# Feed-forward stage: POOL takes over the last norm's variances, and ACT applies the norm two blocks later

## The chip, the cores and the metric

The kernel runs on one core of a Trainium2 chip. It is one program of 54,028 instructions on five engines that run side by side and meet through semaphores: PE (matrix multiply), DVE (vector), ACT (activation), POOL (GpSimd) and SP, which here only issues transfers. The metric is the device time of one execution in microseconds (us). Three runs of the kernel before gave 1488.28, 1488.96 and 1490.38 us, median 1488.96.

## The reference

A decoder layer on 64 sequences of 64 tokens with 256 channels (4096 tokens): self-attention, cross-attention and a feed-forward part, each added to the residual and followed by a layer norm. Only the feed-forward part and the last norm matter here:

```python
def _quant_act(x):
    scale = jnp.maximum(jnp.max(jnp.abs(x), axis=-1, keepdims=True), EPS) / 127.0
    xq = jnp.clip(jnp.round(x / scale), -128.0, 127.0) * scale
def bitlinear(x, w):                      # _quant_weight: ternary weights
    return jnp.einsum('bsi,oi->bso', _quant_act(x), _quant_weight(w))
gate = jax.nn.sigmoid(bitlinear(x, w_gate))   # 256 -> 1024
up = bitlinear(x, w_up)
h = gate * up
return bitlinear(h, w_down)                   # 1024 -> 256
# then: x = _layernorm(x + ffn(x)), v = var(x), (x - m) / sqrt(v + 1e-5)
```

## The kernel before

`feed_forward` is the last stage of the program. It works on 32 blocks of 128 tokens (NB = 32), one token per partition. X holds the residual, `X[:, e, :]` is block e, 128x256 in f32. There is no loop on the chip: every engine has its own straight list of instructions, written slot by slot. Slot n handles block n in its first step and earlier blocks in the later steps. What an engine does in a slot, in this order (line numbers are those of the kernel before):

- PE: `gP` and `uP` of block n (L1501), the down projection `xprojP` of block n-3 (L1511), the transposes `hmP` of block n-2 (L1520).
- ACT: `sig` of block n (L1543), `ds` = scaled down projection of n-3 (L1549), `hqT` of n-2 (L1554), and the last norm of an older block in place, `X*rstd + shift` (L1568). The list NORMED says which: block n-10, and in the last slot, 35, what is left of blocks 0 to 27.
- DVE: `hs` = up times gate of block n (L1644), its maximum `hsc` (L1647), the reciprocal `hinv` (L1649), and for block n-4 the statistics of the last norm, `bn_stats` (L1679) and `bn_aggr` (L1681). `bn_stats` leaves six numbers per token: count, mean and sum of squared deviations for two halves of the row; `bn_aggr` makes mean and variance of them (`ln_moments`).
- POOL: the residual add `X` for block n-3 (L1592); for block n the clipped reciprocal `hinv` (L1595), the quantised hidden row `hm` (L1598), the scale `hsc` (L1599) and the down scale `dsc` (L1601). Some slots have more: 1, 2, 12 and 13 have two `f_xs` each (L1617), slot 5 has the four small steps of the norm before (L1605 to L1610), and every fourth slot from 7 on calls `roots` for a group of four blocks.

`roots(m)` of group m, blocks 4m to 4m+3, stands in slot 4m+7, at its end. It has four instructions on 128x4 tiles: variance plus eps (L1578), power -0.5 (L1580), minus the mean (L1582), times the root (L1585). The groups 0 to 6 are blocks 0 to 27. The blocks 28 to 30 (group 7) and 31 (group 8) are done at the end, with only the first two instructions, and DVE applies their norm (L1692).

SP issues one output transfer for a group, in order of the groups (L1634): each waits for the norm of its whole group, and the ones behind it wait for SP.

Double buffers tie the engines together: `hs` of block n waits for `hm` of block n-2, the POOL's `hinv` of block n waits for DVE's reciprocal of block n, `hmP` waits for `hm`, and `uP` of block n waits for `hs` of block n-1.

Of the kernel before, what the change touches and what calls it, by code (L numbers as in the profile page):

```python
# [5 lines left out]
F32 = mybir.dt.float32  # L6
# [1438 lines left out]
def feed_forward(nc, X, ffn, projP, out, sem, sb, part):  # L1445
# [9 lines left out]
    tP = [part.enter_context(nc.psum_tensor(n, [P, DFF], F16)) for n in ("hmP0", "hmP1")]  # L1455
    dP = [projP[:, i * TILE:(i + 1) * TILE] for i in range(2)]
    s_g, s_u, s_t, s_dn = (sem("f_" + n) for n in ("g", "u", "t", "dn"))
    s_sig, s_h, s_max, s_sc, s_inv, s_dsc, s_hm, s_te, s_ds, s_y = (sem("f_" + n) for n in (
        "sig", "h", "max", "sc", "inv", "dsc", "hm", "te", "ds", "y"))
    s_stats, s_mom, s_rstd, s_normed, s_out = (sem("f_" + n) for n in ("stats", "mom", "rstd", "normed", "out"))  # L1460
    GROUP = 4
    groups = [slice(i, i + GROUP) for i in range(0, NB - GROUP, GROUP)] + [slice(NB - GROUP, NB - 1), slice(NB - 1, NB)]
# [26 lines left out]
    with nc.Block() as block:  # L1489
# [45 lines left out]
        @block.scalar  # L1535
        def _(act):
            def slot(n, has):
                if n == NB - PB:
                    wait(act, s_last, GUSC)
                if has(0):  # L1540
                    wait(act, s_g, n + 1)
                    wait(act, s_h, n - 1)
                    nc.scalar.activation(sig[:, n % 2, :], gP[:, :], ACT.Sigmoid, scale=gsc[:, n:n + 1]).then_inc(s_sig, 1)  # L1543
                if has(3) and n - 3 < LATE:
                    e = n - 3
                    wait(act, s_dn, e + 1)
# [13 lines left out]
                if 6 <= n < 6 + PB:  # L1560
                    i = NB - PB + n - 6
                    x = X[:, i, :]
                    wait(act, s_lastp, SHIFT)
                    nc.scalar.activation(x, x, ACT.Identity, bias=shift[:, i:i + 1], scale=rstd[:, i:i + 1]).then_inc(s_xqT, 1)
                for e in NORMED[n]:
                    x = X[:, e, :]
                    wait(act, s_shift, e // GROUP + 1)
                    nc.scalar.activation(x, x, ACT.Identity, bias=shift[:, e:e + 1], scale=rstd[:, e:e + 1]).then_inc(s_by_act, 1)  # L1568

            NORMED = [[e for e in range(MAIN) if min(e + 10, NB + 3) == n] for n in range(NB + 4)]  # L1570
            blocks(slot, 4)

        @block.gpsimd
        def _(pool):
            def roots(m):
                own = groups[m]
                wait(pool, s_mom, own.stop)
                nc.gpsimd.tensor_scalar(rstd[:, own], moments[:, own, 1], EPS, None, ALU.add).then_inc(s_small, 1)  # L1578
                wait(pool, s_small, 2 * m + 2 - max(0, m - MAIN // GROUP))
                nc.gpsimd.tensor_tensor(rstd[:, own], rstd[:, own], power[:, 0:own.stop - own.start], ALU.pow).then_inc(s_rstd, 1)  # L1580
                if own.stop <= MAIN:
                    nc.gpsimd.tensor_scalar(shift[:, own], moments[:, own, 0], -1.0, None, ALU.mult).then_inc(s_small, 1)  # L1582
                    wait(pool, s_small, 2 * m + 3)
                    wait(pool, s_rstd, m + 1)
                    nc.gpsimd.tensor_tensor(shift[:, own], shift[:, own], rstd[:, own], ALU.mult).then_inc(s_shift, 1)  # L1585

            def slot(n, has):
                if has(3) and n - 3 < LATE:
                    e = n - 3
                    wait(pool, s_ds, e + 1)  # L1590
                    x = X[:, e, :]
                    nc.gpsimd.tensor_tensor(x, ds[:, e % 2, :], x, ALU.add).then_inc(s_y, 1)  # L1592
                if has(0):
                    wait(pool, s_inv, n + 1)
                    nc.gpsimd.tensor_scalar(hinv[:, n:n + 1], hinv[:, n:n + 1], 1.0 / EPS, 127.0, ALU.min, ALU.mult).then_inc(s_sc, 1)  # L1595
                    wait(pool, s_sc, 2 * n + 1)
                    wait(pool, s_t, n - 1)
                    nc.gpsimd.tensor_scalar(hm[:, n % 2, :], hs[:, n % 2, :], hinv[:, n:n + 1], MAGIC16, ALU.mult, ALU.add).then_inc(s_hm, 1)  # L1598
                    nc.gpsimd.tensor_scalar(hsc[:, n:n + 1], hsc[:, n:n + 1], EPS, 1.0 / 127.0, ALU.max, ALU.mult).then_inc(s_sc, 1)  # L1599
                    wait(pool, s_sc, 2 * n + 2)  # L1600
                    nc.gpsimd.tensor_tensor(dsc[:, n:n + 1], hsc[:, n:n + 1], wsc[:, 2:3], ALU.mult).then_inc(s_dsc, 1)  # L1601
                if n == 5:
                    own = last_tile
                    wait(pool, s_last, MOM[PB - 1])
                    nc.gpsimd.tensor_scalar(rstd[:, own], moments[:, own, 1], EPS, None, ALU.add).then_inc(s_lastp, 1)  # L1605
                    nc.gpsimd.tensor_scalar(shift[:, own], moments[:, own, 0], -1.0, None, ALU.mult).then_inc(s_lastp, 1)
                    wait(pool, s_lastp, EPS2)
                    nc.gpsimd.tensor_tensor(rstd[:, own], rstd[:, own], power[:, :], ALU.pow).then_inc(s_lastp, 1)
                    wait(pool, s_lastp, ROOT)
                    nc.gpsimd.tensor_tensor(shift[:, own], shift[:, own], rstd[:, own], ALU.mult).then_inc(s_lastp, 1)  # L1610
                for k, tile in enumerate(XS_AT):
                    if n in XS_AT[tile]:
                        wait(pool, s_last, XINV if k else 0)
                        first = XS_AT[tile].index(n) * PB // 2
                        for b in range(first, first + PB // 2):
                            i = tile * PB + b
                            nc.gpsimd.tensor_scalar(xs[:, k, b, :], X[:, i, :], xinv[:, i:i + 1], MAGIC16, ALU.mult, ALU.add).then_inc(s_lastp, 1)  # L1617
                for m in range(NG):
                    if n - 4 == groups[m].stop - 1:
                        roots(m)  # L1620

# [123 lines left out]
```

## Time and profile before

| | us |
|---|---|
| median of three runs | 1488.96 |
| time of the profiled execution | 1488.86 |
| its span (first to last event) | 1486.8 |
| feed-forward stage | from 1364.3 to the end, 122.5 |
| busy over the whole span: PE, DVE, ACT, POOL | 1375.3, 1196.8, 1256.0, 1269.5 |

The profile counts all times from the start of the span. The busy shares of the whole program average three different stages; the change touches only the last 8% of the time, so the stage must be read by itself, from stretches, waits and the instructions in order of time. A start-to-start distance between two instructions of one engine says what the first one costs there; the printed duration alone does not, since the next one may start before it ends or a little after.

### The profile page before, as it was taken

To read this page: it belongs to the slowest core of one execution; us is meant where nothing else is said; L and a number is where in the kernel's file an instruction comes from. 1 tells how busy PE (TensorE), PEld (TensorE's weight loads), DVE (VectorE), ACT (ScalarE), POOL (GpSimd) and SP (SyncE) were. 2 spreads that over 40 slices of the span, in tenths; PEclk is the share of its full clock that TensorE was granted. 3 is DMA by queue.
4 is the path that set the end of the run, shared out by engine and by line. 5 is a ranking of instruction groups with operands and counts; after the bars stand their busy time and mean duration, and the time that the engine had idled before them with its cause. 6 is when DMAs were issued, how large, how long until landed. Compare 5 with 4: busy or idle time off the path is not lost. (4 is left out here: it accounts for less than half of the span.)

```text
span 1486.8 us, 54028 instructions
## 1 busy us (share of the span) xinstructions
PE 1375.3 (93%) x19830; PEld 1031.8 (69%) x20034; DVE 1196.8 (80%) x2796; ACT 1256.0 (84%) x4059; POOL 1269.5 (85%) x1307
## 2 busy tenths in 40 slices
PE   6999999999999999999999999868999999987897
PEld 3677777777777777777777777636777777765554
DVE  4887887887888878788787777878888888874997
ACT  6888888888888888888888888769999999996797
POOL 5889999999889899899898898658888899883887
PEclk9999999999999999999999999989999999999999
DMA  7700000000000000000000000023443433330012
GB/s 257 193 8 31 31 3 31 22 11 31 3 31 31 3 31 31 2 31 23 11 17 3 17 3 2 6 72 94 115 111 112 111 94 96 99 87 1 1 44 71
DMA packets 58132, 73.25 MB, mean 49 GB/s; under 512 B 14320, under 2 KB 41776, under 8 KB 57872
## 3 DMA queue, kind: packets, MB, share of 16 engines
q1 hardware_dynamic: 57872, 69.79, 15.7%
q8 instruction: 162, 2.65, 0.7%
q14 instruction: 98, 0.80, 0.2%
HBM read 32.54 MB, written 4.19 MB: 25 GB/s over the span
## 5 line engine op out<-in xcount | busy, mean ns | idle before, releaser
L663 DVE SCALAR_TENSOR_TENSOR X<-projP,r,X 128x256 f32<-128x256 f32 x512 | 211.2, 475 | 0.1
L305 PEld LDWEIGHTS svP<-W,xT 128*128 128x128 bf16 x3072 | 182.4, 98 | 31.9 <-DVE scores L650 2.5
L305 PE MATMUL svP<-W,xT 128*128 128x128 bf16 x3072 | 192.9, 219 | 0.4 <-DVE scores L650 0.4
L739 POOL TENSOR_TENSOR y_sql<-y_sq 128x512 bf16<-128x512 f32 x128 | 133.5, 1043 | 66.7 <-ACT y_sq L466 66.4
L256 PE MATMUL qkssP<-xT,W 128*128 128x512 bf16 x641 | 161.7, 383 | 29.5 <-issue 20.0
L256 PE MATMUL kP<-xT,W 128*128 128x512 bf16 x768 | 188.6, 382 | 0.2 <-DVE kl L696 0.2
L481 ACT ACTIVATE probs<-scores,ntop 128x64 f32<-128x64 f32 x512 | 170.5, 339 | 9.6 <-DVE ntop L653 9.6
L336 PE MATMUL projP<-W,y 128*128 128x256 bf16 x1024 | 175.9, 274 | 2.1 <-POOL yl L739 2.1
L1230 ACT ACTIVATE x_probs<-xsP,x_ntop 128x64 f32<-128x64 f32 x512 | 152.2, 325 | 19.3 <-DVE x_ntop L1307 18.5
L739 POOL TENSOR_TENSOR k_sql<-moved_k 128x512 bf16<-128x512 f32 x128 | 135.7, 1060 | 24.5 <-ACT moved_k L492 23.5
L938 POOL TENSOR_TENSOR qhl<-qh 128x1024 bf16<-128x1024 f32 x64 | 121.2, 1893 | 34.3 <-issue 23.3
L779 POOL TENSOR_TENSOR KVl<-q 128x512 bf16<-128x512 f32 x128 | 145.5, 1137 | 0.0
L336 PE MATMUL projP<-W,yl 128*128 128x256 bf16 x512 | 140.2, 274 | 0.0
L256 PEld LDWEIGHTS kP<-xT,W 128*128 128x128 bf16 x768 | 75.5, 98 | 92.8 <-issue 3.0
L739 POOL TENSOR_TENSOR q_sql<-turned_k 128x512 bf16<-128x512 f32 x128 | 133.0, 1039 | 3.2 <-ACT turned_k L473 3.2
L782 POOL TENSOR_TENSOR vl<-v 128x512 bf16<-128x512 f32 x128 | 135.6, 1059 | 0.0
L739 POOL TENSOR_TENSOR yl<-y 128x512 bf16<-128x512 f32 x128 | 133.0, 1039 | 0.0
L256 PEld LDWEIGHTS qkssP<-xT,W 128*128 128x128 bf16 x768 | 65.1, 98 | 77.6 <-issue 11.6
L672 DVE COPY v<-svP 128x512 f32<-128x512 f32 x128 | 88.3, 690 | 34.4 <-PE svP L305 34.0
L650 DVE SCALAR_TENSOR_TENSOR scores<-svP,r,bias 128x64 f32<-128x64 f32 x512 | 110.0, 277 | 4.5
L691 DVE TENSOR_TENSOR ptl<-pyP,pth 128x256 bf16<-128x256 f32 x128 | 54.3, 424 | 72.9 <-ACT pth L427 70.6
L1230 ACT ACTIVATION_READ_ACCUMULATOR x_probs<-xsP,x_ntop 128x1 f32 x512 | 111.6, 218 | 0.0
(281 smaller groups left out, 4890.9 us busy)
## 6 DMA issues: line engine op xcount, KB each, us to landing
x_turned<-x_turn SPq DMA_DIRECT2D x128, 128.0 KB, 2.1
oB<-oA SPq DMA_DIRECT2D x232, 64.0 KB, 2.0
w_stage<-in_wqkvp SPq DMA_DIRECT2D x16, 512.0 KB, 3.6
x_stage<-in_xT SPq DMA_DIRECT2D x8, 512.0 KB, 4.1
X<-in_x SPq DMA_DIRECT2D x1, 4096.0 KB, 16.8
x_stage<-in_ctxT SPq DMA_DIRECT2D x8, 512.0 KB, 4.2
out<-X SPq DMA_DIRECT2D x7, 512.0 KB, 3.0
okv<-in_L_xattn_W_o SPq DMA_DIRECT2D x1, 2048.0 KB, 12.0
```

The source lines that it names most:

```text
L256: last = nc.tensor.matmul(dst[:, :], weight(parity, u, i, c), xT[:, z, c, tok], start=(c == 0 and k == 0), stop=(c == CC - 1 and k == 2))
L305: last = nc.tensor.matmul(svP[:, b * D:(b + 1) * D], xT[:, u, c, t * TILE + b * P:t * TILE + (b + 1) * P], weight(parity, z, 2, c), start= ...
L336: last = nc.tensor.matmul(projP[:, b * C:(b + 1) * C], y_part, W[:, (j - 3) // NT % 2, z, 3 * CC * D:], start=(i == 0), stop=(i == 2))
L481: last = nc.scalar.activation(probs[:, b, :], scores[:, b, :], ACT.Exp, bias=ntop[:, b:b + 1], accum_out=total[:, b:b + 1])
L650: last = nc.vector.scalar_tensor_tensor(scores[:, b, :], svP[:, b * T:(b + 1) * T], r[:, b:b + 1], row, ALU.mult, ALU.add)
L663: last = nc.vector.scalar_tensor_tensor(acc, projP[:, b * C:(b + 1) * C], r[:, PB + b:PB + b + 1], acc, ALU.mult, ALU.add)
L672: nc.vector.tensor_copy(v[:, j % 4, :], svP[:, :]).then_inc(s_ve, 1)
L739: return nc.gpsimd.tensor_tensor(dst[:, :], src[:, :], high(src, slice(None), 0, TILE), ALU.subtract)
L779: nc.gpsimd.tensor_tensor(ql[:, j % 2, :], q[:, j % 2, :], high_of(q, j % 2), ALU.subtract).then_inc(s_ql, 1)
L782: nc.gpsimd.tensor_tensor(vl[:, j % 4, :], v[:, j % 4, :], high_of(v, j % 4), ALU.subtract).then_inc(s_vl, 1)
L938: return eng.tensor_tensor(dst, src, high_part(src), ALU.subtract)
L1230: last = nc.scalar.activation(probs[:, m % 3, b % PB, b // PB, :], sP[:, b * T:(b + 1) * T], ACT.Exp, bias=ntop[:, b:b + 1], accum_out=tot ...
```

## The change

The second half of the norm's statistics moves. DVE no longer runs `bn_aggr` for blocks 0 to 27 of the last norm; it only runs `bn_stats`. POOL works the variance out for four blocks at a time, straight from the six numbers per token: `sums` (three instructions, at the end of slot 4m+7), `variances` (four, slot 4m+8) and `roots` (three, slot 4m+9). They compute four times the variance and the negative double mean, and correct the factors at the end. The blocks 28 to 31 keep `bn_aggr` and the old steps under the name `last_roots`.

The steps of the POOL for each block become one fewer: `hsc` and `dsc` are one instruction, with the constant `wsc/127` made once at the start (`wdc`). ACT applies the norm to block n-12 in place of block n-10. The semaphores `s_max` and `s_inv` become one, `s_top`; that changes no order.

```diff
-            NORMED = [[e for e in range(MAIN) if min(e + 10, NB + 3) == n] for n in range(NB + 4)]
+            NORMED = [[e for e in range(MAIN) if min(e + 12, NB + 3) == n] for n in range(NB + 4)]
@@ POOL
+            def sums(m):
+                own = groups[m]
+                st = stats[:, own, :]
+                wait(pool, s_stats, own.stop)
+                nc.gpsimd.tensor_tensor(gap[:, own], st[:, :, 1], st[:, :, 4], ALU.subtract).then_inc(s_small, 1)
+                nc.gpsimd.tensor_tensor(shift[:, own], st[:, :, 1], st[:, :, 4], ALU.add).then_inc(s_small, 1)
+                nc.gpsimd.tensor_tensor(rstd[:, own], st[:, :, 2], st[:, :, 5], ALU.add).then_inc(s_small, 1)
+            def variances(m):
+                own = groups[m]
+                wait(pool, s_small, 7 * m + 5)
+                nc.gpsimd.tensor_scalar(rstd[:, own], rstd[:, own], 4.0 / C, 4.0 * EPS, ALU.mult, ALU.add).then_inc(s_small, 1)
+                nc.gpsimd.tensor_tensor(gap[:, own], gap[:, own], gap[:, own], ALU.mult).then_inc(s_small, 1)
+                nc.gpsimd.tensor_scalar(shift[:, own], shift[:, own], -1.0, None, ALU.mult).then_inc(s_small, 1)
+                wait(pool, s_small, 7 * m + 8)
+                nc.gpsimd.tensor_tensor(rstd[:, own], rstd[:, own], gap[:, own], ALU.add).then_inc(s_small, 1)
             def roots(m):
                 own = groups[m]
-                wait(pool, s_mom, own.stop)
-                nc.gpsimd.tensor_scalar(rstd[:, own], moments[:, own, 1], EPS, None, ALU.add).then_inc(s_small, 1)
-                wait(pool, s_small, 2 * m + 2 - max(0, m - MAIN // GROUP))
+                wait(pool, s_small, 7 * m + 9)
+                nc.gpsimd.tensor_tensor(rstd[:, own], rstd[:, own], power[:, :], ALU.pow).then_inc(s_rstd, 1)
+                wait(pool, s_rstd, m + 1)
+                nc.gpsimd.tensor_tensor(shift[:, own], shift[:, own], rstd[:, own], ALU.mult).then_inc(s_shift, 1)
+                wait(pool, s_shift, 2 * m + 1)
+                nc.gpsimd.tensor_scalar(rstd[:, own], rstd[:, own], 2.0, None, ALU.mult).then_inc(s_shift, 1)
...
-                    nc.gpsimd.tensor_scalar(hsc[:, n:n + 1], hsc[:, n:n + 1], EPS, 1.0 / 127.0, ALU.max, ALU.mult).then_inc(s_sc, 1)
-                    wait(pool, s_sc, 2 * n + 2)
-                    nc.gpsimd.tensor_tensor(dsc[:, n:n + 1], hsc[:, n:n + 1], wsc[:, 2:3], ALU.mult).then_inc(s_dsc, 1)
+                    nc.gpsimd.tensor_scalar(dsc[:, n:n + 1], hsc[:, n:n + 1], EPS, wdc[:, 0:1], ALU.max, ALU.mult).then_inc(s_dsc, 1)
...
                 for m in range(NG):
-                    if n - 4 == groups[m].stop - 1:
-                        roots(m)
+                    end = groups[m].stop - 1
+                    if end < MAIN:
+                        for lag, part_ in enumerate((sums, variances, roots)):
+                            if n - 4 - lag == end:
+                                part_(m)
+                    elif n - 4 == end:
+                        last_roots(m)
@@ DVE
                     nc.vector.bn_stats(stats[:, e, :], X[:, e, :]).then_inc(s_stats, 1)
-                    wait(dve, s_stats, e + 1)
-                    nc.vector.bn_aggr(moments[:, e, :], stats[:, e, :]).then_inc(s_mom, 1)
+                    if e >= MAIN:
+                        wait(dve, s_stats, e + 1)
+                        nc.vector.bn_aggr(moments[:, e, :], stats[:, e, :]).then_inc(s_mom, 1)
```

POOL, one group in the middle of the stage, before: the end of one slot with the group's work, and the start of the next slot.

```order
L1598 TENSOR_SCALAR hm<-hs,hinv 128x1024
L1599 TENSOR_SCALAR hsc<-hsc 128x1
L1601 TENSOR_TENSOR dsc<-hsc,wsc 128x1
L1578 TENSOR_SCALAR ln_rstd<-ln_moments 128x4
L1580 TENSOR_TENSOR ln_rstd<-ln_rstd,ln_power 128x4
L1582 TENSOR_SCALAR ln_shift<-ln_moments 128x4
L1585 TENSOR_TENSOR ln_shift<-ln_shift,ln_rstd 128x4
L1592 TENSOR_TENSOR X<-ds,X 128x256
```

The four instructions of L1578 to L1585 are the whole group; after them come three slots that have none.

POOL, the same group after the change, over three slots (`ln_gap` is the difference of the two half means):

```order
L1626 TENSOR_SCALAR dsc<-hsc,wdc 128x1
L1581 TENSOR_TENSOR ln_gap<-ln_stats 128x4
L1582 TENSOR_TENSOR ln_shift<-ln_stats 128x4
L1583 TENSOR_TENSOR ln_rstd<-ln_stats 128x4
...
L1590 TENSOR_SCALAR ln_rstd<-ln_rstd 128x4
L1591 TENSOR_TENSOR ln_gap<-ln_gap 128x4
L1592 TENSOR_SCALAR ln_shift<-ln_shift 128x4
L1594 TENSOR_TENSOR ln_rstd<-ln_rstd,ln_gap 128x4
...
L1600 TENSOR_TENSOR ln_rstd<-ln_rstd,ln_power 128x4
L1602 TENSOR_TENSOR ln_shift<-ln_shift,ln_rstd 128x4
L1604 TENSOR_SCALAR ln_rstd<-ln_rstd 128x4
```

Ten small instructions stand where four stood, and each of the four slots has one small instruction fewer. Where a row is only "...", the four instructions of a slot (X, hinv, hm, dsc) are left out.

ACT, the end of its list before, from its last `hqT` but one:

```order
L1554 ACTIVATE hqT<-hmP 128x1024
L1568 ACTIVATE X<-X,ln_shift,ln_rstd 128x256
L1554 ACTIVATE hqT<-hmP 128x1024
L1568 ACTIVATE X<-X,ln_shift,ln_rstd 128x256 x5
```

and after the change:

```order
L1555 ACTIVATE hqT<-hmP 128x1024
L1569 ACTIVATE X<-X,ln_shift,ln_rstd 128x256
L1555 ACTIVATE hqT<-hmP 128x1024
L1569 ACTIVATE X<-X,ln_shift,ln_rstd 128x256 x7
```

Two more norms stand behind the last `hqT`: blocks 21 to 27 in place of 23 to 27.

## Rows read from the trace of the kernel before

**Rows 1.** Stretch: PE, PEld, DVE, ACT, POOL busy us (count), granted clock, DMA share, GB/s.
```profile
1440.00:1453.00 13.00, 12.88 (x96) 7.63 (x96) 12.53 (x21) 11.92 (x17) 11.37 (x25) 1.00 0.13 42
```

**Rows 2.** Waits from 1364 to 1487: total us, times, longest.
```profile
POOL hinv L1595 <- DVE hinv L1649: 7.2, 4, 5.1
...
DVE hs L1644 <- POOL hm L1598: 0.7, 2, 0.5
```

**Rows 3.** POOL in order of time, one group: start us, us, instruction.
```profile
1424.80 0.19 POOL L1601 TENSOR_TENSOR dsc<-hsc,wsc 128x1 f32<-128x1 f32 x1
1424.95 0.24 POOL L1578 TENSOR_SCALAR ln_rstd<-ln_moments 128x4 f32<-128x4 f32 x1
1425.27 1.04 POOL L1580 TENSOR_TENSOR ln_rstd<-ln_rstd,ln_power 128x4 f32<-128x4 f32 x1
1426.40 0.25 POOL L1582 TENSOR_SCALAR ln_shift<-ln_moments 128x4 f32<-128x4 f32 x1
1426.73 0.20 POOL L1585 TENSOR_TENSOR ln_shift<-ln_shift,ln_rstd 128x4 f32<-128x4 f32 x1
1426.88 0.72 POOL L1592 TENSOR_TENSOR X<-ds,X 128x256 f32<-128x256 f32 x1
...
1429.69 0.73 POOL L1592 TENSOR_TENSOR X<-ds,X 128x256 f32<-128x256 f32 x1
...
1432.02 0.22 POOL L1599 TENSOR_SCALAR hsc<-hsc 128x1 f32<-128x1 f32 x1
1432.33 0.19 POOL L1601 TENSOR_TENSOR dsc<-hsc,wsc 128x1 f32<-128x1 f32 x1
1432.47 0.73 POOL L1592 TENSOR_TENSOR X<-ds,X 128x256 f32<-128x256 f32 x1
...
1438.03 0.24 POOL L1578 TENSOR_SCALAR ln_rstd<-ln_moments 128x4 f32<-128x4 f32 x1
```

**Rows 4.** DVE in order of time, the end of a slot.
```profile
1428.87 0.41 DVE L1679 BATCH_NORM_STATS2 ln_stats<-X 128x6 f32<-128x256 f32 x1
1429.31 0.18 DVE L1681 BATCH_NORM_AGGREGATE ln_moments<-ln_stats 128x2 f32<-128x6 f32 x1
1429.41 1.28 DVE L1644 SCALAR_TENSOR_TENSOR hs<-uP,usc,sig 128x1024 f32<-128x1024 f32 x1
...
1432.62 1.28 DVE L1644 SCALAR_TENSOR_TENSOR hs<-uP,usc,sig 128x1024 f32<-128x1024 f32 x1
```

**Rows 5.** POOL's last waits for DVE, and two neighbours without a wait.
```profile
1393.90 0.23 POOL L1595 TENSOR_SCALAR hinv<-hinv 128x1 f32<-128x1 f32 x1 [0.99 <-DVE hinv L1649]
...
1409.30 0.24 POOL L1578 TENSOR_SCALAR ln_rstd<-ln_moments 128x4 f32<-128x4 f32 x1 [0.28 <-DVE ln_moments L1681]
...
1414.20 1.05 POOL L1617 TENSOR_SCALAR f_xs<-X,xinv 128x256 f16<-128x256 f32 x2
1415.33 0.73 POOL L1592 TENSOR_TENSOR X<-ds,X 128x256 f32<-128x256 f32 x1
```

**Rows 6.** The end of the stage, all engines in order of time.
```profile
1467.29 1.12 POOL L1598 TENSOR_SCALAR hm<-hs,hinv 128x1024 f16<-128x1024 f32 x1
...
1469.12 1.02 ACT L1554 ACTIVATE hqT<-hmP 128x1024 bf16<-128x1024 f16 x1 [0.28 <-PE hmP L1520]
...
1475.62 1.12 POOL L1598 TENSOR_SCALAR hm<-hs,hinv 128x1024 f16<-128x1024 f32 x1
...
1477.85 1.02 ACT L1554 ACTIVATE hqT<-hmP 128x1024 bf16<-128x1024 f16 x1 [1.10 <-PE hmP L1520]
...
1478.77 2.60 ACT L1568 ACTIVATE X<-X,ln_shift,ln_rstd 128x256 f32<-128x256 f32 x5
...
1480.87 0.18 DVE L1681 BATCH_NORM_AGGREGATE ln_moments<-ln_stats 128x2 f32<-128x6 f32 x1
...
1482.38 1.38 DVE L1692 TENSOR_SCALAR X<-X,ln_moments,ln_rstd 128x256 f32<-128x256 f32 x4 [0.81 <-POOL ln_rstd L1580]
```

**Rows 7.** The last six microseconds with transfers (columns as rows 1).
```profile
1480.00:1486.00 6.00, 0.00 (x0) 0.00 (x0) 2.88 (x9) 1.36 (x3) 1.93 (x4) 0.66 0.77 262
```

More of the change, by code:

```diff
@@ L1457, in feed_forward @@
     s_g, s_u, s_t, s_dn = (sem("f_" + n) for n in ("g", "u", "t", "dn"))
-    s_sig, s_h, s_max, s_sc, s_inv, s_dsc, s_hm, s_te, s_ds, s_y = (sem("f_" + n) for n in (
-        "sig", "h", "max", "sc", "inv", "dsc", "hm", "te", "ds", "y"))
+    s_sig, s_h, s_top, s_sc, s_dsc, s_hm, s_te, s_ds, s_y = (sem("f_" + n) for n in (
+        "sig", "h", "top", "sc", "dsc", "hm", "te", "ds", "y"))
     s_stats, s_mom, s_rstd, s_normed, s_out = (sem("f_" + n) for n in ("stats", "mom", "rstd", "normed", "out"))
@@ L1466, in feed_forward @@
     s_small, s_shift = sem("f_small"), sem("f_shift")
+    gap, wdc = sb("ln3_gap", [P, NB], F32), sb("wdc", [P, 1], F32)
     s_by_act = sem("f_byact")
@@ L1566, in slot @@
                     x = X[:, e, :]
-                    wait(act, s_shift, e // GROUP + 1)
+                    wait(act, s_shift, 2 * (e // GROUP + 1))
                     nc.scalar.activation(x, x, ACT.Identity, bias=shift[:, e:e + 1], scale=rstd[:, e:e + 1]).then_inc(s_by_act, 1)
-            NORMED = [[e for e in range(MAIN) if min(e + 10, NB + 3) == n] for n in range(NB + 4)]
+            NORMED = [[e for e in range(MAIN) if min(e + 12, NB + 3) == n] for n in range(NB + 4)]
             blocks(slot, 4)
@@ L1578, in roots, with last_roots @@
+            def last_roots(m):
+                own = groups[m]
+                wait(pool, s_mom, own.stop - MAIN)
                 nc.gpsimd.tensor_scalar(rstd[:, own], moments[:, own, 1], EPS, None, ALU.add).then_inc(s_small, 1)
-                wait(pool, s_small, 2 * m + 2 - max(0, m - MAIN // GROUP))
+                wait(pool, s_small, 7 * (MAIN // GROUP) + 3 + m - MAIN // GROUP)
                 nc.gpsimd.tensor_tensor(rstd[:, own], rstd[:, own], power[:, 0:own.stop - own.start], ALU.pow).then_inc(s_rstd, 1)
[L1581 to L1585, printed above, removed]
@@ L1593, in slot @@
                 if has(0):
-                    wait(pool, s_inv, n + 1)
+                    wait(pool, s_top, 2 * n + 2)
                     nc.gpsimd.tensor_scalar(hinv[:, n:n + 1], hinv[:, n:n + 1], 1.0 / EPS, 127.0, ALU.min, ALU.mult).then_inc(s_sc, 1)
-                    wait(pool, s_sc, 2 * n + 1)
+                    wait(pool, s_sc, n + 1)
                     wait(pool, s_t, n - 1)
                     nc.gpsimd.tensor_scalar(hm[:, n % 2, :], hs[:, n % 2, :], hinv[:, n:n + 1], MAGIC16, ALU.mult, ALU.add).then_inc(s_hm, 1)
-                    nc.gpsimd.tensor_scalar(hsc[:, n:n + 1], hsc[:, n:n + 1], EPS, 1.0 / 127.0, ALU.max, ALU.mult).then_inc(s_sc, 1)
-                    wait(pool, s_sc, 2 * n + 2)
-                    nc.gpsimd.tensor_tensor(dsc[:, n:n + 1], hsc[:, n:n + 1], wsc[:, 2:3], ALU.mult).then_inc(s_dsc, 1)
+                    nc.gpsimd.tensor_scalar(dsc[:, n:n + 1], hsc[:, n:n + 1], EPS, wdc[:, 0:1], ALU.max, ALU.mult).then_inc(s_dsc, 1)
                 if n == 5:
@@ L1618, in slot @@
                 for m in range(NG):
-                    if n - 4 == groups[m].stop - 1:
-                        roots(m)
+                    end = groups[m].stop - 1
[5 more added lines that the diff above has]
+                        last_roots(m)
             nc.gpsimd.memset(power[:, :], -0.5).then_inc(s_small, 1)
-            pool.wait_ge(s_small, 1)
+            nc.gpsimd.tensor_scalar(wdc[:, :], wsc[:, 2:3], 1.0 / 127.0, None, ALU.mult).then_inc(s_small, 1)
+            pool.wait_ge(s_small, 2)
             blocks(slot, 4)
@@ L1646, in slot @@
                     wait(dve, s_h, n + 1)
-                    nc.vector.tensor_reduce(hsc[:, n:n + 1], hs[:, n % 2, :], AX, ALU.max, apply_absolute_value=True).then_inc(s_max, 1)
-                    wait(dve, s_max, n + 1)
-                    nc.vector.reciprocal(hinv[:, n:n + 1], hsc[:, n:n + 1]).then_inc(s_inv, 1)
+                    nc.vector.tensor_reduce(hsc[:, n:n + 1], hs[:, n % 2, :], AX, ALU.max, apply_absolute_value=True).then_inc(s_top, 1)
+                    wait(dve, s_top, 2 * n + 1)
+                    nc.vector.reciprocal(hinv[:, n:n + 1], hsc[:, n:n + 1]).then_inc(s_top, 1)
                 if 1 <= n < 1 + PB:
```

## The prediction

> **What bounds the kernel now.** I read four views, all of the feed-forward stage alone, since nothing else changes. First the busy times by stretch [rows 1]: in a 13 us stretch of the middle PE, DVE, ACT and POOL are busy 12.9, 12.5, 11.9 and 11.4 us, so the busy share names no bound; POOL even looks like the freest. The clock is 1.00, TensorE's upper level, and drops out. Second the waits [rows 2]: POOL waits for DVE's reciprocal only 4 times in 32 blocks, and DVE waits for POOL's `hm` twice. Third POOL in order of time [rows 3], where the question is decided. A plain slot goes from `X` at 1429.69 to `X` at 1432.47, 2.78 us. A slot's end with the four group instructions has 1.93 us more (1424.95 to 1426.88). Four slots and one group are 4 x 2.78 + 1.93 = 13.05 us, and the group's first instruction comes back after 1438.03 - 1424.95 = 13.08 us. Nothing is left over: POOL is never idle there. Its low busy time is the gaps of 0.08 us between its instructions, which the summary counts as idle. Its last real waits are at 1393.90 (0.99 us) and at 1409.30 (0.28 us) [rows 5]; from there to the end of the last `hm` at 1475.62 + 1.12 = 1476.74 [rows 6] it runs through. Fourth DVE [rows 4]: 3.21 us from `hs` to `hs`, 12.84 us for four blocks. So POOL bounds the second half of the stage, with DVE only 0.24 us behind in 13.08. The change takes work from the second and gives work to the first.
>
> **DVE's part.** `bn_aggr` goes 28 times. Now 0.54 us pass from `bn_stats` to `hs` (1428.87 to 1429.41) [rows 4]. Without the aggregate, `hs` can start when `bn_stats` (0.41) is done, at the earliest 0.08 before its printed end, as `hs` now starts 0.08 before the printed end of the aggregate (1429.31 + 0.18 - 1429.41). That is 0.13 to 0.21 us per block, DVE's block becomes 3.0 us and four of them 12.0 us. Where POOL sets the pace this is worth nothing: DVE waits for `hm` instead. It counts only in slots 4 to 6, where POOL still waits for DVE. Together with the shorter POOL slots there I take -0.3 us for the start of POOL's `hinv` in slot 7 (now at 1393.90), between 0 and -0.8 (three blocks' gain of 0.2 and POOL's own 0.14).
>
> **POOL's slot.** `hsc` to `dsc` is 0.31 us (1432.02 to 1432.33), `dsc` to `X` 0.14 (1432.33 to 1432.47) [rows 3]. One of the two instructions goes. The one that stays is a tensor_scalar, followed by `X`. What such a neighbourhood costs the trace shows at `f_xs`, a tensor_scalar followed by `X`: 1414.20 + 1.05 = 1415.25, and `X` starts at 1415.33, a gap of 0.08 [rows 5]. So the new `dsc` costs 0.22 + 0.08, about 0.31, and the slot falls from 2.78 to 2.64: -0.14. The other end: if `X` may start 0.05 before its predecessor's printed end, as it does behind the old `dsc`, it is -0.27. I take -0.14, for the row with the same kind of instruction. From slot 7 to slot 30 that is 24 x 0.14 = -3.4 us.
>
> **POOL's group.** Before 1.93 us. After, from the same rows [rows 3]: a small tensor_tensor is 0.20 (L1585) and gets 0.09 behind it where nothing shortens it (L1580, 1.04, to L1582: 1.13), and 0.15 start to start where `X` follows (1426.73 to 1426.88). A small tensor_scalar with its successor is 0.33 (L1582 to L1585).
> `sums`: 0.29 + 0.29 + 0.15 = 0.73. `variances`: 0.33 + 0.29 + 0.33 + 0.15 = 1.10. `roots`: power 1.13, product 0.29, doubling 0.33 = 1.75. Together 3.58 us, which is +1.65 per group. The power, 1.04 of the old 1.93, stays. Six groups (0 to 5) lie before the last `hm`: +9.9 us. The bounds: with tensor_tensors that follow each other at 0.15 in place of 0.29 (three places) it is +1.2 per group; if reading every sixth number makes each new instruction 0.05 us longer it is +2.15. No row shows either, and I stay with the middle.
>
> At this place a rule of the Trainium skill speaks for the cheap end. GPSIMD Engine Reference, section 2.1 (Instruction dispatch), says that completion holds back only what waits on the instruction's semaphore, and that each of the eight cores goes on to the next instruction when its own share is done. Then neighbours that don't depend on each other should overlap. The trace agrees behind the old `dsc` (0.14 after a 0.19 instruction) and disagrees between L1580 and L1582, which are independent and stand 0.09 apart. The sum by the rule is the second rival.
>
> The new group of four slots is then 4 x 2.64 + 3.58 = 14.14 us against 13.08 now and 12.0 for DVE. POOL is the bound by 2.1 us per group, so also from slot 8 on, where DVE still set the pace in part; the 0.28 us wait at 1409.30 is swallowed (-0.3). The waits inside the new steps are for POOL's own instructions just before, and are in the 0.33 and 0.29. `hinv`, `hm`, `dsc` and `X` of the next slot are queued behind them, and DVE's `hs` two blocks on, PE's transposes and ACT's `hqT` wait for `hm`: the whole stage takes POOL's pace. ACT's norm, 12 behind, needs the roots of slot 4m+9 in its own slot 4m+12, behind an `hqT` that needs the later `hm` of slot 4m+10; it never waits before the end. Moving the norm costs ACT nothing in the middle.
>
> **The sum to the last `hm`.** -0.3 + 9.9 - 3.4 - 0.3 = +5.9: it ends at 1482.6 and not 1476.74.
>
> **The tail.** Now `hqT` of block 31 starts 1.11 us after the end of its `hm` (1477.85), because PE is still at the block before. Where POOL sets the pace it takes 0.71 (`hm` 1467.29 + 1.12, `hqT` 1469.12) [rows 6]: -0.4. The dependent part to the end then shifts by +5.5. Behind it stands the output. POOL still has to do `dsc` and all three steps of group 6 after the last `hm`: 0.08 + 0.31 + 3.58 = 4.0 us. ACT's four norms of 0.52 (2.60 / 5) end at 6.05 after the `hm`; today the last ACT norm ends at 1481.37, 4.6 after it. SP issues in order, so 1 MB (groups 6, 7 and 8) leaves from 6.05 on. The end of the span, 1486.8, stands 1486.8 - 1476.74 - 0.4 = 9.7 us behind a POOL-bound `hm`. At 262 GB/s [rows 7] 1 MB takes 4.0 us. Today the last, 128 KB, takes 3.0 us from the end of DVE's norm (1483.76), of which its data are 0.5; with all of the other 2.5 in line the output would end at 12.6, +2.9; with the transfers fully hidden in each other, +0. I take +1.2, since most of the 2.5 is the way from the last packet to its notice and from the issue to the first, which the busy 262 GB/s stretch hides in part. The last three blocks' roots come out even: the statistics of block 30 are done at 1481.05, 3.9 after such an `hm`, and POOL is free at 4.0.
>
> **Total.** +5.5 + 1.2 = +6.7 on the profiled execution's 1488.86 (its span 1486.8 and 2.06 around it), which stands 0.1 under the median of the runs: 1495.5 us.
>
> **Rivals.**
> 1. *POOL-bound, gaps charged* (the forecast), 1495.5. For it: 13.08 against 13.05 in the sum of rows.
> 2. *POOL-bound, but small neighbours overlap.* Slot -0.27 and group +1.2: against the forecast -24 x 0.13 - 6 x 0.42 = -5.6, so 1489.9, no measurable change. For it: the 0.14 behind the old `dsc`. Against it: the `f_xs` row and L1580.
> 3. *DVE was the true pace, and POOL follows.* If the new POOL group fits into DVE's 12.0 us, the stage loses 0.2 us in 28 blocks, 5.6 us, and the output costs its 1.2 back: 1484.5, faster. It decides from a POOL group under 13.08. Plain slots are 4 x 2.64 = 10.56, so the ten new instructions would have to take under 2.5 us, and 1.04 is the power alone; even in rival 2 they take 3.1 with a slot of 2.51, 13.2 in all. Little speaks for it beyond the busy sums [rows 1], where DVE is 1.2 us busier than POOL.
> 4. *The new instructions are longer than their likes.* 60 of them at +0.05: +3.0, 1498.5. Strided reads and a scale read from a tile have no row here.
>
> The Trainium skill has a rule against the direction of the whole change: GPSIMD Engine Reference, section 4.1 (Engine selection), gives elementwise work to VectorE. In this trace one `bn_aggr` costs DVE about 0.2 us, four of them 0.8, and their replacement costs POOL 1.65.
>
> **How the numbers follow.** Chances: forecast 0.60, rival 2 0.20, rival 4 0.13, rival 3 0.07. This kernel's time can be told from no change from about 0.2% on, 3 us. Rivals 1 and 4 are slower (0.73), rival 2 is the same (0.20), rival 3 faster (0.07). The range is 1489.5 to 1498.5: it takes in the forecast, nearly all of rival 4 and the upper half of rival 2, and leaves out rival 3. The forecast's own range is 1492.5 to 1497.5, from the bounds of the tail (0 to 2.9) and of the slot.
>
> **What would show it.** Right: POOL's group first instruction returns every 14.1 us, `dsc` to `X` is 0.31, `sums`, `variances` and `roots` take 0.7, 1.1 and 1.75; POOL has no wait for DVE from slot 8 on; DVE shows a wait for `hm` of about 0.5 us in each slot; the last `hm` ends near 1482.6; the last ACT norms wait for `ln_rstd`. Wrong: POOL waits for `hinv` in the middle of the stage (rival 3), a group period near 13.2 (rival 2), or a last output that ends less than 9.7 us after the last `hm`.

## The result and the profile after

The changed kernel is slower: a median of 1492.18 us (1491.4 to 1497.15) against 1488.14 (1485.33 to 1490.38), 14 runs each; the ratio is 1.0036, 95% interval 1.0027 to 1.0046, which is +5.4 us (+4.0 to +6.8). The two medians alone are 4.0 us apart: eight of the changed kernel's executions lie at 1491.4 to 1492.4, six at 1493.4 to 1497.2, and the profiled one (1491.89) is one of the eight, so that what the six have more is seen in no trace. The forecast was 1495.5 with a range of 1489.5 to 1498.5.

The span of the profiled execution grew by 3.3 us, 1486.8 to 1490.1. Part of that is chance: the feed-forward stage began 1.28 us earlier in this execution (DVE's first `X` at 1363.08, before at 1364.36), though nothing ahead of it was changed. So I compare inside the stage, from that `X` on:

| us | before | after | difference |
|---|---|---|---|
| start of the stage to the end of the last `hm` | 112.38 | 115.74 | +3.36 |
| end of the last `hm` to the start of DVE's last residual add | 3.27 | 4.11 | +0.84 |
| from there to the end of the span | 6.79 | 7.17 | +0.38 |
| stage | 122.44 | 127.02 | +4.58 |

One group in the middle, POOL of the kernel after, in order of time (start us, us, instruction), answering to [rows 3]:

```profile
1423.87 0.30 POOL L1626 TENSOR_SCALAR dsc<-hsc,wdc 128x1 f32<-128x1 f32 x1
1424.13 0.20 POOL L1581 TENSOR_TENSOR ln_gap<-ln_stats 128x4 f32<-128x4 f32 x1
1424.28 0.20 POOL L1582 TENSOR_TENSOR ln_shift<-ln_stats 128x4 f32<-128x4 f32 x1
1424.44 0.20 POOL L1583 TENSOR_TENSOR ln_rstd<-ln_stats 128x4 f32<-128x4 f32 x1
1424.59 0.73 POOL L1619 TENSOR_TENSOR X<-ds,X 128x256 f32<-128x256 f32 x1
...
1427.33 0.20 POOL L1590 TENSOR_SCALAR ln_rstd<-ln_rstd 128x4 f32<-128x4 f32 x1
1427.61 0.20 POOL L1591 TENSOR_TENSOR ln_gap<-ln_gap 128x4 f32<-128x4 f32 x1
1427.90 0.24 POOL L1592 TENSOR_SCALAR ln_shift<-ln_shift 128x4 f32<-128x4 f32 x1
1428.23 0.20 POOL L1594 TENSOR_TENSOR ln_rstd<-ln_rstd,ln_gap 128x4 f32<-128x4 f32 x1
1428.38 0.73 POOL L1619 TENSOR_TENSOR X<-ds,X 128x256 f32<-128x256 f32 x1
...
1431.01 1.04 POOL L1600 TENSOR_TENSOR ln_rstd<-ln_rstd,ln_power 128x4 f32<-128x4 f32 x1
1432.12 0.20 POOL L1602 TENSOR_TENSOR ln_shift<-ln_shift,ln_rstd 128x4 f32<-128x4 f32 x1
1432.42 0.24 POOL L1604 TENSOR_SCALAR ln_rstd<-ln_rstd 128x4 f32<-128x4 f32 x1
1432.64 0.73 POOL L1619 TENSOR_TENSOR X<-ds,X 128x256 f32<-128x256 f32 x1
...
1444.78 1.04 POOL L1600 TENSOR_TENSOR ln_rstd<-ln_rstd,ln_power 128x4 f32<-128x4 f32 x1
```

The power comes back after 1444.78 - 1431.01 = 13.77 us, before 13.08. `sums` takes 0.46 us to the next `X`, `variances` 1.05, `roots` 1.63. The `dsc` is 0.26 in front of `X` or a tensor_tensor (1423.87 to 1424.13).

The waits of the stage (total us, times, longest), answering to [rows 2]:

```profile
POOL hinv L1622 <- DVE hinv L1680: 8.2, 6, 4.9
PEld hmP L1521 <- POOL hm L1625: 7.0, 8, 1.8
PE hmP L1521 <- POOL hm L1625: 5.1, 5, 1.5
DVE hs L1675 <- POOL hm L1625: 4.8, 4, 1.2
```

DVE waited 0.7 us for `hm` before, now 4.8; PE 5.1. POOL's `hinv` still waits for DVE, but up to slot 12 only, the last time for 0.20 us at 1409.22.

DVE's slot where it sets its own pace, early in the stage, answering to [rows 4], and the first of four waits of 1.2 us, one in each group:

```profile
1381.14 1.28 DVE L1675 SCALAR_TENSOR_TENSOR hs<-uP,usc,sig 128x1024 f32<-128x1024 f32 x1
1383.79 0.41 DVE L1710 BATCH_NORM_STATS2 ln_stats<-X 128x6 f32<-128x256 f32 x1
1384.12 1.27 DVE L1675 SCALAR_TENSOR_TENSOR hs<-uP,usc,sig 128x1024 f32<-128x1024 f32 x1
...
1421.27 1.28 DVE L1675 SCALAR_TENSOR_TENSOR hs<-uP,usc,sig 128x1024 f32<-128x1024 f32 x1 [1.22 <-POOL hm L1625]
```

The slot is 2.98 us (1381.14 to 1384.12) and was 3.21: the relief of DVE is real, 0.23 us, and is spent waiting.

The end of the stage, PE, ACT, DVE and POOL in order of time, answering to [rows 6], and PE's clock in two stretches (columns as [rows 1]):

```profile
1476.26 0.62 PE L1521 MATMUL hmP<-identh,hm 128*128 128x128 f16 x8 [1.50 <-POOL hm L1625]
...
1477.70 1.12 POOL L1625 TENSOR_SCALAR hm<-hs,hinv 128x1024 f16<-128x1024 f32 x1
...
1477.99 1.89 PE L1512 MATMUL xprojP<-wd,hqT 128*128 128x256 bf16 x8 [1.12 <-ACT hqT L1555]
...
1479.67 1.06 PE L1521 MATMUL hmP<-identh,hm 128*128 128x128 f16 x8
...
1480.77 1.02 ACT L1555 ACTIVATE hqT<-hmP 128x1024 bf16<-128x1024 f16 x1 [2.35 <-PE hmP L1521]
...
1481.69 3.54 ACT L1569 ACTIVATE X<-X,ln_shift,ln_rstd 128x256 f32<-128x256 f32 x7
...
1482.93 0.48 DVE L1706 SCALAR_TENSOR_TENSOR X<-xprojP,dsc,X 128x256 f32<-128x256 f32 x1 [1.98 <-PE xprojP L1512]
```

```profile
1476.00:1477.00 1.00, 0.62 (x8) 0.45 (x8) 0.00 (x0) 0.09 (x1) 0.89 (x3) 1.00 0.64 212
...
1478.00:1479.00 1.00, 1.00 (x5) 0.72 (x6) 0.43 (x2) 0.42 (x1) 0.90 (x2) 0.50 0.00 0
```

The granted clock is 1.00 to 1477 and 0.50 (TensorE's 1.2 GHz level) in 1478 to 1480. PE had stood still for 1.50 us before 1476.26, waiting for `hm`, and for 1.12 us before 1477.99, waiting for `hqT`. The eight matmuls of `xprojP` then take 1.89 us and not 1.05, the eight of `hmP` 1.06 and not 0.62. Before, the clock stayed at 1.00 until all matmuls were done; the last eight there:

```profile
1479.00:1480.00 1.00, 0.97 (x8) 0.62 (x8) 0.00 (x0) 1.00 (x3) 0.20 (x1) 1.00 0.00 0
```

### The profile page after: what moved, and what is told of

Its sections match the earlier page's. It is cut to its first block and busy times, and to the rows that moved or that the text cites. A ratio compares the mean times of both kernels' runs of the same rounds, so it can differ in the third digit from the quotient of the medians.

```text
span 1490.1 us, 54208 instructions
## 1 busy us (share of the span) xinstructions
PE 1403.3 (94%) x20034; PEld 1031.7 (69%) x20034; DVE 1192.3 (80%) x2768; ACT 1256.3 (84%) x4059; POOL 1273.6 (85%) x1318
## 3 DMA queue, kind: packets, MB, share of 16 engines
q8 instruction: 162, 2.65, 0.7%
## 5 line engine op out<-in xcount | busy, mean ns | idle before, releaser
L256 PE MATMUL qkssP<-xT,W 128*128 128x512 bf16 x768 | 190.4, 384 | 9.1 <-POOL W L744 8.0
L938 POOL TENSOR_TENSOR qhl<-qh 128x1024 bf16<-128x1024 f32 x64 | 121.2, 1893 | 33.5 <-issue 22.6
## 6 DMA issues: line engine op xcount, KB each, us to landing
x_turned<-x_turn SPq DMA_DIRECT2D x128, 128.0 KB, 2.1
```

What stands on the lines that cost most here:

```text
L256: last = nc.tensor.matmul(dst[:, :], weight(parity, u, i, c), xT[:, z, c, tok], start=(c == 0 and k == 0), stop=(c == CC - 1 and k == 2))
L938: return eng.tensor_tensor(dst, src, high_part(src), ALU.subtract)
```

## The experiments

Stage lengths are read like the table above, from each profiled execution. The same kernel run twice (E2 and E10) gave 121.4 and 122.2. The traces show where the 0.8 us lie. PE stands still for 2.5 to 2.7 us ahead of the stage's first matmul in all twelve executions. In seven of them (E4 to E10) the granted clock then fell to 0.50 while the first blocks ran, and `hm` of block 2 started 11.77 to 12.21 us after the start of the stage; in the other five (before, after, E1 to E3) it stayed at 1.00 and that took 11.28 to 11.33. PE's first blocks in E2 and in E10 (columns as [rows 1]):

```profile
1362.00:1364.00 2.00, 1.66 (x8) 0.51 (x6) 0.95 (x2) 1.11 (x1) 0.00 (x0) 1.00 0.00 0
1364.00:1366.00 2.00, 2.00 (x6) 0.63 (x5) 0.04 (x2) 1.11 (x1) 0.00 (x0) 0.50 0.00 0
```

So the table also gives a stretch that leaves out the start and the end: from the start of `hm` of block 2 to the start of `hm` of block 31. Its beginning in the kernel before and in the changed one (the ends are at 1475.62 [rows 6] and 1477.70 above):

```profile
1375.69 1.12 POOL L1598 TENSOR_SCALAR hm<-hs,hinv 128x1024 f16<-128x1024 f32 x1
1374.36 1.12 POOL L1625 TENSOR_SCALAR hm<-hs,hinv 128x1024 f16<-128x1024 f32 x1
```

It repeats to 0.03 us (before and E3, E2 and E10) where the clock doesn't fall on the way. It fell there in E6 and E9, as told below, and in E1 from 1417.5 to 1420.9, where no block took visibly longer. The sharper verdicts rest on it and on the periods in the middle, which repeat within 0.05 us. Each ratio is to executions of the kernel before taken beside that kernel.

| kernel | period of a group | `hm` of block 2 to `hm` of block 31 | stage | ratio to before (95%) |
|---|---|---|---|---|
| before | 13.08 | 99.93 | 122.4 | |
| after | 13.77 | 103.34 | 127.0 | 1.0036 (1.0027 to 1.0046) |
| E1 two steps | 14.41 | 107.22 | 130.6 | 1.0050 (1.0038 to 1.0062) |
| E2 merge only | 12.82 | 98.49 | 121.4 | 0.9985 (0.9977 to 0.9994) |
| E3 lag only | 13.08 | 99.90 | 122.8 | 0.9997 (0.9988 to 1.0005) |
| E4 DVE keeps | 13.80 | 104.31 | 128.0 | 1.0033 (1.0021 to 1.0044) |
| E5 double sums | 14.22 | 105.97 | 132.0 | 1.0055 (1.0040 to 1.0069) |
| E6 free variance | 12.5 | 97.68, clock fell | 121.2 | 0.9979 (0.9971 to 0.9987) |
| E7 relief only | 13.08 | 99.47 | 122.5 | 0.9995 (0.9987 to 1.0004) |
| E8 late aggregate | 12.56 | 98.28 | 121.8 | 0.9993 (0.9985 to 1.0002) |
| E9 spread | 12.42 | 98.98, clock fell | 122.0 | 0.9995 (0.9987 to 1.0004) |
| E10 merge again | 12.82 | 98.48 | 122.2 | 0.9995 (0.9986 to 1.0004) |

**E1, two steps.** The changed kernel, with

```diff
-nc.gpsimd.tensor_scalar(dsc[...], hsc[...], EPS, wdc[:, 0:1], ALU.max, ALU.mult)
+nc.gpsimd.tensor_scalar(hsc[...], hsc[...], EPS, 1.0 / 127.0, ALU.max, ALU.mult)
+wait(pool, s_sc, 2 * n + 2)
+nc.gpsimd.tensor_tensor(dsc[...], hsc[...], wsc[:, 2:3], ALU.mult)
```

> The changed kernel with the two POOL instructions hsc and dsc put back in place of the merged one. Theory (POOL sets the pace of the stage from slot 8 on): the trace of the changed kernel has a plain POOL slot of 2.62 us, the kernel before 2.78, so 24 slots up to the last hm are 0.16 us longer each: +3.8 us over the changed kernel, +8 to +9 over the kernel before, and the period of the POOL's group goes from 13.8 to 14.4 us. Rival (DVE's or PE's pace rules, POOL only follows): no difference from the changed kernel.

The power of L1600 starts at 1431.06 and again at 1445.46:

```profile
1431.06 1.04 POOL L1600 TENSOR_TENSOR ln_rstd<-ln_rstd,ln_power 128x4 f32<-128x4 f32 x1
1445.46 1.04 POOL L1600 TENSOR_TENSOR ln_rstd<-ln_rstd,ln_power 128x4 f32<-128x4 f32 x1
```

14.40 us, the forecast period, and from block 2 to block 31 it is 3.88 us over the changed kernel, 3.8 expected. A POOL instruction that costs 0.16 us in each slot lies on the path in full. In the time the two kernels are 2 us apart (1.0050 and 1.0036), and the intervals overlap.

**E5, double sums.** The changed kernel with the three instructions of `sums` issued once more into a spare tile.

> The changed kernel with the three instructions of sums issued a second time per group into a spare tile (nobody reads it). In the trace of the changed kernel sums takes 0.46 us (1424.13 to 1424.59) start to start. Theory (every instruction of POOL's group lies on the path): period of the group 13.77 + 0.46 = 14.2 us, +2.8 us up to the last hm over the changed kernel (6 groups), and another 0.5 us in front of the last group's roots. Rival (the added POOL work is in part hidden by the waits for DVE): less than half of that.

Period 14.22 (+0.45), and 2.63 us more from block 2 to block 31, 2.8 expected. The rest of its +4.9 us of stage is 0.85 at the start and 1.45 behind the last `hm`: in this execution the clock was 0.50 at both places.

**E4, DVE keeps.** The changed kernel with

```diff
-                    if e >= MAIN:
-                        wait(dve, s_stats, e + 1)
-                        nc.vector.bn_aggr(moments[:, e, :], stats[:, e, :]).then_inc(s_mom, 1)
+                    wait(dve, s_stats, e + 1)
+                    last = nc.vector.bn_aggr(moments[:, e, :], stats[:, e, :])
+                    if e >= MAIN:
+                        last.then_inc(s_mom, 1)
```

> The changed kernel with bn_aggr put back on DVE for blocks 0 to 27, its result read by nobody; POOL works as in the changed kernel. Theory (DVE's relief is worth nothing, since DVE only waits for hm): the same as the changed kernel, up to +0.6 us from slots 4 to 6, and DVE's waits for hm shrink from about 4.8 us. Rival (DVE's relief is worth its 28 x 0.13 to 0.21 us and POOL's additions hide it): +3.6 to +5.9 us over the changed kernel.

The ratio is that of the changed kernel, 1.0033 against 1.0036, and the period is 13.80 against 13.77. From block 2 to block 31 it took 0.97 us more, above my 0.6: 0.23 before block 7, 0.55 from there to block 12, 0.19 in the nineteen blocks behind. So DVE sets the pace in more of the first slots than 4 to 6. DVE's waits for `hm` shrank from 4.8 us to 3.7. In the middle the relief of DVE is worth 0.03 us in a period, next to nothing.

**E7, relief only.** The kernel before, its DVE without `bn_aggr` for blocks 0 to 27, whose moments are set once to 1.

> The kernel before, unmerged, without bn_aggr for blocks 0 to 27 (their moments set once to 1; this part of the last norm is not computed). Theory: POOL keeps its 13.08 us per group and sets the pace, so DVE's relief is worth only what it gives in the first third, where POOL waits for DVE: 0 to -1.5 us. Rival (DVE was the bound of the kernel before): -4 to -6 us.

Ratio 0.9995 and the old period of 13.08. From block 2 to block 31 it is 0.46 us less than before, all but 0.02 of it ahead of block 13: no gain where POOL sets the pace. DVE's waits for `hm` in the stage:

```profile
DVE hs L1645 <- POOL hm L1599: 2.4, 4, 0.6
```

2.4 us against 0.7 in [rows 2]. Here nothing was added to POOL, so this refutes my third rival directly: DVE was not the bound of the kernel before.

**E2, merge only.** The kernel before, with only the one-instruction `dsc` of the change.

> The kernel before with only hsc and dsc merged into one POOL instruction; DVE keeps bn_aggr, POOL keeps the old four-instruction roots, the norm is 10 behind. Theory: POOL's four slots and group need 4 x 2.62 + 1.93 = 12.4 us, less than DVE's 12.84, so the bound passes from POOL (13.08) to DVE and only the difference is gained: 0.24 us in each of 5 groups, -1.2 us, with the slots ahead of them -1 to -2 us against the kernel before. Rival A (POOL's pace counts in full, DVE is not next): 0.64 per group, -3.4 us. Rival B (POOL never was the bound): 0.

The period is 12.82, DVE's own 4 x 3.21, and POOL now waits for DVE often:

```profile
POOL hinv L1596 <- DVE hinv L1649: 11.3, 11, 4.9
```

11 times and not 4 [rows 2]. From block 2 to block 31 it is 1.44 us less than before, inside the 1 to 2 expected. Ratio 0.9985 here, 0.9995 (0.9986 to 1.0004) in the repetition:

> The merged-dsc kernel a second time, unchanged, on the same chip as the kernel of the spread f_xs, for the comparison of the two. Expected: 0.9985 of the kernel before again, a stage of 121.4 us.

So the bound did pass from POOL to DVE, and the gain up to the last `hm` is what was expected, in both executions. In the time it is between nothing and 0.2%, and the repetition alone can't tell it from no change.

**E6, free variance.** E2 without `bn_aggr` for blocks 0 to 27.

> The merged-dsc kernel (DVE still with bn_aggr, POOL with the old roots) without bn_aggr for blocks 0 to 27: their moments are set once to 1, so this part of the last norm is not computed; everything else is. It shows what the relief of DVE would be worth if the variances cost nothing elsewhere. Theory: with POOL at 12.4 us per four slots, DVE was next at 12.84 and now needs 12.0; the loop of ACT and PE comes next at about 3.14 us per slot, 12.55 (in the changed kernel hs to hs is 3.15 where nobody waits for POOL). So 0.3 us in each of 6 groups and 0.2 in the slots ahead: -1.5 to -2.5 us against the merged-dsc kernel. Rival (DVE's relief counts in full at 0.2 a block): -5 us or more.

The period fell to 12.43 to 12.57, and DVE's longest group of waits is now for ACT:

```profile
DVE hs L1645 <- ACT sig L1544: 6.6, 12, 2.2
```

From block 2 to block 31 it is 0.81 us less than E2. But in this execution the granted clock fell to 0.50 at 1394, while PE's matmuls ran on behind a standstill of 1.54 us, and blocks 7 to 12 took 19.08 us where E2 took 17.85. Outside of them it is 2.04 us less than E2, inside the 1.5 to 2.5 expected. The ratio, 0.9979, is 0.9 us under E2's, and the two intervals overlap. This kernel's is the least time that the whole idea could give if the variances were free: with POOL and DVE both relieved, the next limit (by DVE's waits, the loop through PE and ACT) stands 0.3 us behind in a group.

**E3, lag only.** The kernel before with `min(e + 12, NB + 3)` in NORMED.

> The kernel before with only the norm on ACT 12 blocks behind in place of 10. Theory: nothing changes up to the last hm; behind it ACT has seven norms after its last hqT in place of five, so the outputs of blocks 20 to 27 leave 1.0 us later, in front of the same last transfers: +0.4 us (0 to +1.2). Rival (the two added slots of distance free ACT of waits in the middle): -1 us or more; the trace of the kernel before shows no wait of ACT for ln_shift there, so I don't expect it.

No measurable change, period 13.08. From DVE's last residual add to the end 7.19 us against 6.79, the +0.4 expected; the five executions with the norm 10 behind (before, E2, E6, E7, E10) lie at 6.77 to 6.87.

**E8, late aggregate, and E9, spread.** E2 with the roots one slot later, the norm 11 blocks behind, and on DVE

```diff
+                    if 1 <= e < MAIN:
+                        wait(dve, s_stats, e)
+                        nc.vector.bn_aggr(moments[:, e - 1, :], stats[:, e - 1, :]).then_inc(s_mom, 1)
                     nc.vector.bn_stats(stats[:, e, :], X[:, e, :]).then_inc(s_stats, 1)
-                    wait(dve, s_stats, e + 1)
-                    nc.vector.bn_aggr(moments[:, e, :], stats[:, e, :]).then_inc(s_mom, 1)
+                    if e >= MAIN - 1:
+                        wait(dve, s_stats, e + 1)
+                        nc.vector.bn_aggr(moments[:, e, :], stats[:, e, :]).then_inc(s_mom, 1)
```

> The merged-dsc kernel with bn_aggr of block e-1 in front of bn_stats of block e, so that it doesn't wait for a result just written (before: 0.44 us from bn_stats to bn_aggr, of which 0.33 are needed if the next instruction doesn't depend on it); POOL's roots one slot later for groups 0 to 5 and ACT's norm 11 blocks behind for blocks 0 to 23. Theory: DVE's slot falls from 3.21 to 3.10, and the loop of ACT and PE at about 3.14 takes over: -0.07 x 20 slots = -1.4 us (0 to -2) against the merged-dsc kernel. Rival (the distance is set by something else than the dependence): 0.

The period did fall, 12.82 to 12.56, but from block 2 to block 31 only 0.2 us came of it, of 1.4 expected (0 to 2), and the time did not move. Between 1417.25 and 1430.92 one group took 13.67: POOL's slot 12 held the roots of group 1 and two `f_xs`. E9 moves the `f_xs` (slots 13 and 14, PE's transposes in 16).

> The late-aggregate kernel with the two pairs of f_xs in slots 13 and 14 in place of 12 and 13, and their transposes on PE in slot 16 in place of 15. In the late-aggregate kernel POOL's slot 12 held both the roots of group 1 (now one slot late) and a pair of f_xs, and the stage lost there what its 12.55 us groups gained later (13.67 us from the power at 1417.25 to the next at 1430.92). Theory: the pile is gone, about 1 us of it comes back, and the stage is 120.6 to 121.0 us long, against 121.4 in the merged-dsc kernel and 121.8 in the late-aggregate one. Rival (the loss at that place is not the pile): 121.8 again.

The periods are the best of all, 12.42, but the stage was 122.0 and the ratio 0.9995. The trace shows that chance took part in this. Up to slot 12 the two kernels are the same, and PE stands still for 1.54 us at the same instruction in both. In E8 the granted clock stayed at 1.00 behind it, in E9 it fell to 0.50 (first the two lines of E8, then those of E9):

```profile
1393.41 1.04 PE L1502 MATMUL gP<-wg,xqT 128*128 128x512 bf16 x4 [1.54 <-ACT sig L1544]
1394.00:1397.00 3.00, 2.72 (x24) 1.72 (x22) 2.93 (x6) 2.45 (x4) 1.68 (x4) 1.00 0.02 5
1389.96 1.04 PE L1502 MATMUL gP<-wg,xqT 128*128 128x512 bf16 x4 [1.54 <-ACT sig L1544]
1392.00:1395.00 3.00, 3.00 (x17) 2.04 (x16) 2.93 (x6) 1.11 (x2) 1.64 (x3) 0.50 0.02 5
```

Blocks 7 to 12 took 18.81 us in E9 and 17.64 in E8. From block 12 to block 31 E9 is 0.46 us less (61.98 and 62.44): about half of the expected 1 us did come back. Still, E9 is only 0.24 under E2 there (62.22), with periods that are 0.4 shorter. One `hs` starts 4.67 us after the one before it, with DVE waiting for ACT:

```profile
1421.61 1.28 DVE L1644 SCALAR_TENSOR_TENSOR hs<-uP,usc,sig 128x1024 f32<-128x1024 f32 x1 [0.17 <-POOL hm L1599]
1426.28 1.28 DVE L1644 SCALAR_TENSOR_TENSOR hs<-uP,usc,sig 128x1024 f32<-128x1024 f32 x1 [1.54 <-ACT sig L1544]
```

Most of what the shorter periods gain is lost around the second set of `f_xs` transposes and ACT's copy of them, in both orders. Why it is that much I did not settle. None of these versions is surely better than E2.

## Why the prediction was right, point by point

**POOL is the bound: right.** E7 and E4 take or give DVE its 28 aggregates and the period stays (13.08, 13.80); E1 and E5 give POOL 0.16 us a slot or 0.45 a group and the period follows by 0.64 and 0.45.

**The slot, -0.14: right.** 2.65 us from `X` to `X` behind the roots (1432.64 to 1435.29 in the trace after), where the kernel before has 2.81 (1426.88 to 1429.69) [rows 3]: -0.16. A slot that does not follow the roots went from 2.78 to 2.62. The new `dsc` is longer than its kind, 0.30 and not 0.22, but `X` starts 0.04 before its end. I had taken 0.22 and a gap of 0.08, two errors that nearly cancel; that the term came out to 0.02 us is in part luck.

**The group, +1.65: the mis-sized term.** It is 0.46 + 1.05 + 1.63 = 3.14, and 0.13 for the later start of `variances` behind `dsc` (0.39 and not 0.26), 3.27 in all against my 3.58: +1.34. Most of the error is `sums`, 0.46 against 0.73. I gave two of three tensor_tensors 0.29 start to start; all three take 0.155. In `roots` the doubling takes 0.22 to `X` and not 0.33 (1432.42 to 1432.64). The rule of the Trainium skill that I had put at the cheap end (GPSIMD Engine Reference, section 2.1, Instruction dispatch) agrees with `sums`, whose three don't depend on each other, and with L1602, which does depend on L1600 and starts 0.07 behind its end. Independence is not all of it, since L1591 to L1592, independent as well, stand 0.29 apart. From L1600 the next starts 1.11 later, about as taken. The range of +1.2 to +2.15 held the value, in its lower third.

**The start, -0.3: right.** `hinv` of slot 7 is 29.17 us after the start of the stage (1392.25 - 1363.08), before 29.54: -0.37. The clock stood at 1.00 at the start of both, and -0.32 of it lies between `hm` of block 2 and `hm` of block 7 (18.53 to 18.21).

**The sum to the last `hm`, +5.9: +3.36.** The smaller group gives -0.31 x 6 = -1.9, the slots -0.02 x 24 = -0.5; together with +5.9 that is +3.5.

**The tail, +0.8: +1.2, by another way; that it came near is luck.** I expected -0.4 to DVE's last residual add and +1.2 behind it. In E1 and E4 it went so: 2.88 us from the last `hm` to the add (before 3.27), then 8.08 and 7.92 (before 6.79). ACT waits there for the last doubling:

```profile
1481.88 0.48 DVE L1706 SCALAR_TENSOR_TENSOR X<-xprojP,dsc,X 128x256 f32<-128x256 f32 x1 [1.59 <-PE xprojP L1512]
...
1482.82 2.07 ACT L1569 ACTIVATE X<-X,ln_shift,ln_rstd 128x256 f32<-128x256 f32 x4 [0.62 <-POOL ln_rstd L1604]
```

(E4, in order of time.) In the changed kernel's execution PE fell to the lower clock first. That cost 1.2 us (4.11 - 2.88; the sixteen matmuls alone took 0.84 and 0.44 more), hid ACT's wait and 0.8 of the output's, and left +1.2. I had dropped the clock out of the argument because it stood at 1.00 in the middle; the step that failed is that a slower POOL leaves PE waiting at the end, and that was not looked at. E1 and E4 had gaps of 1.65 and 1.10 us before PE's transposes at the end and kept the clock at 1.00, so the gap alone doesn't decide it. By the way I had expected, the tail of E1 and E4 cost 0.9 and 0.7 us.

**The signs.** The period was 13.77 and not 14.1, nearer to the forecast than to the 13.2 of the second rival. DVE does not wait about 0.5 us for `hm` in each slot: it waits 1.2 us in one of four, and in the other three `hs` follows `hs` after 3.13 to 3.20 us without a wait for POOL. And POOL waited for DVE once more, 0.20 us in slot 12, where I had said never from slot 8 on.

**The total.** +4.58 in the stage of one execution and +5.4 (4.0 to 6.8) in the ratio, against +6.7. The median of 1492.18 lies in the stated range, but just under the forecast's own, 1492.5 to 1497.5, since the group was smaller. The likeliest case was right in its mechanism; the cheap neighbours of the second rival hold for `sums` and for the doubling, and not for the rest.

## What to carry to other kernels

Ask which engine's chain closes, start to start, over one whole period of the pattern: POOL had the lowest busy time of the four and was the bound, because the gaps of 0.08 us between its small instructions are not counted as busy. Taking work from the engine that is next is worth nothing while it is paid for on the one that rules; here 0.23 us per block on DVE was bought with 0.33 per block on POOL (1.34 / 4). The part of the change that looked like a by-product, one small instruction fewer per block on POOL, was the only one that shortened the period, and its gain ended after 0.26 us in 13.08 at the next engine. And when differences are this small, look at the granted clock of each execution before comparing lengths: the lengths of E6 and E9 alone mislead by over 1 us, until the blocks under the fallen clock are left out.

## What was not expected of the hardware

- Three small tensor_tensors of POOL (128x4) in a row start 0.155 us apart though each is printed as 0.20; a tensor_tensor followed by a tensor_scalar starts 0.29 apart (1427.61 to 1427.90). Six in a row (E5) keep the 0.155.
- Reading every sixth number of a tile costs POOL nothing visible: 0.20 us, like a dense 128x4.
- A tensor_scalar on 128x1 whose second number comes from a tile takes 0.30 us on POOL, with two constants 0.22.
- The granted clock fell to 0.50 at the end, with matmuls still to come, in two kernels: in the changed one after PE had stood still for 1.50 us (to 1476.26) and during its next gap of 1.12, in E5 after gaps of 1.12 and 1.50 (to 1480.00). In E1 and E4, with gaps of 1.65 and 1.10 at the same place and the same 1.12 behind them, it did not.
- At the start of the stage, behind a standstill of PE of 2.5 to 2.7 us, it fell in seven of twelve executions; that alone made the same kernel's stage 0.8 us longer (E2 and E10). In the middle it fell behind a standstill of 1.54 us in E6 and E9 and not in E8, and cost over 1 us. What decides it stays open.
